# Last stage of an eight-layer kernel: four TensorE waits per block left out, gathered blocks in a ring of 12 instead of 8

## The reference

```python
def _L3_ffn_ref(x, gate_w, gate_bias, w1, w3, w2, sw1, sw3, sw2):
    DIM, INTER, N_EXPERTS, TOPK, N_SHARED = 128, 128, 8, 2, 2
    xt = x.reshape(-1, shape[-1])
    scores = jax.nn.softmax((xt @ gate_w.T).astype(jnp.float32), axis=-1)
    _, idx = jax.lax.top_k(scores + gate_bias, TOPK)
    weights = jnp.take_along_axis(scores, idx, axis=1).astype(x.dtype)
    y = jnp.zeros_like(xt)
    for e in range(N_EXPERTS):
        gate_e = jnp.sum(jnp.where(idx == e, weights, 0.0), axis=1)
        h = jax.nn.silu(xt @ w1[e].T) * (xt @ w3[e].T)
        y = y + gate_e[:, None] * (h @ w2[e].T)
    z = jax.nn.silu(xt @ sw1.T) * (xt @ sw3.T) @ sw2.T
    return (y + z).reshape(shape)
...
    x = x + _L3_ffn_ref(_layernorm(x, axis=-1), L3_ffn_gate_w, ...)
```

## Time and profile before

| | |
|---|---|
| three timed runs | 1195.08, 1190.69, 1195.14 us (median 1195.08) |
| the profiled execution's own time | 1197.03 us |
| its span, first to last instruction | 1195.2 us |
| granted TensorE clock, mean over the span | 0.908 of full speed |
| busy share of the span | PE 80%, DVE 70%, ACT 54%, POOL 39% |
| block loop: transpose of block 0 to that of block 58 | 1072.49 to 1182.25 us |

### The profile page before, as it was taken

How to read it: one execution, slowest core, us unless ns; L and a number is a source line. 1 busy time by engine, 2 the same in 40 slices (tenths; PEclk the granted TensorE clock), 3 DMA queues, 4 the chain that set the end, 5 groups by cost and what they waited for, 6 DMA issues and landing times.

```text
span 1195.2 us, 21237 instructions
## 1 busy us (share of the span) xinstructions
PE 957.0 (80%) x7158; PEld 634.0 (53%) x7158; DVE 831.6 (70%) x2062; ACT 647.2 (54%) x1137; POOL 471.0 (39%) x454
## 2 busy tenths in 40 slices
PE   5868810578988998799759999997979988849997
PEld 3653310554555675455416766666735546428876
DVE  5686699857886674477768999999658885414443
ACT  3424567946652444565347878785456644105443
POOL 6610000001120002345169999998012242554544
PEclk9998965679999999999958999999979998969999
DMA  7000000046000000000000000000000000232331
GB/s 281 1 1 1 1 0 0 1 151 185 2 1 1 1 1 1 1 2 2 2 0 1 2 0 0 0 0 1 1 1 1 2 2 1 72 105 77 99 83 47
DMA packets 24234, 33.77 MB, mean 28 GB/s; under 512 B 3484, under 2 KB 20389, under 8 KB 23888
## 3 DMA queue, kind: packets, MB, share of 16 engines
q1 hardware_dynamic: 20720, 26.20, 7.1%
q0 software_dynamic: 3424, 6.38, 1.5%
HBM read 18.34 MB, written 15.98 MB: 29 GB/s over the span
## 4 chain that ended last, share of the span: by engine, by line
issue 71%; PE 6%; DMA 1%; POOL 1%; SPq 0%; POOLq 0%; DVE 0%; ACT 0%; DVEq 0%
PE psum L2417 3%; PE psum L2435 1%; POOL out L2295 1%; DMA out<-big 1%; DMA big<-rows 1%; PE psum L1443 1%; PE psum L2426 1%; PE psum L2410 0%; SPq L2308 0%; POOLq L2291 0%; DVE big L2616 0%; PE psum L289 0%; PE psum L500 0%; ACT hrow L271 0%; PE psum L519 0%
## 5 line engine op out<-in xcount | busy, mean ns | idle before, releaser
L785 DVE TENSOR_REDUCE hq<-psum 128x16 f32<-128x1024 f32 x96 | 114.4, 1221 | 80.5 <-PE psum L519 43.5
L429 POOL TENSOR_TENSOR big<-big,w_const 128x256 f32<-128x256 f32 x48 | 35.8, 748 | 260.6 <-PE psum L565 227.4
L1975 POOL TENSOR_TENSOR big<-big 128x512 f32<-128x512 f32 x128 | 128.7, 1051 | 21.4 <-ACT big L1880 21.4
L1903 ACT ACTIVATE psum<-big,tmp 128x512 f32<-128x512 f32 x128 | 84.9, 686 | 18.9 <-DVE big L2072 16.2
L2072 DVE SCALAR_TENSOR_TENSOR big<-big,tmp,psum 128x512 f32<-128x512 f32 x128 | 90.4, 744 | 5.5 <-ACT psum L1903 2.5
L675 ACT ACTIVATE big<-psum 128x1024 f32<-128x1024 f32 x64 | 62.0, 1021 | 54.4 <-PE psum L549 54.4
L2606 DVE SCALAR_TENSOR_TENSOR big<-psum,big 128x128 f32<-128x128 f32 x118 | 36.0, 348 | 79.2 <-issue 59.9
L790 DVE RECIPROCAL big<-psum 128x256 f32<-128x256 f32 x48 | 84.0, 1750 | 7.5 <-PE psum L565 7.3
L2295 POOL DMA_INDIRECT out<-big x59 | 57.9, 982 | 64.2 <-issue 33.4
L1443 PE MATMUL psum<-f_downT,tmp 128*128 128x128 f32 x192 | 25.7, 300 | 68.0 <-DVE tmp L1326 68.0
L1985 POOL TENSOR_TENSOR big<-big 128x1024 f32<-128x1024 f32 x32 | 75.3, 2366 | 11.4 <-DVE big L2072 11.4
(11 more groups left out here) (316 smaller groups left out, 2584.5 us busy)
## 6 DMA issues: line engine op xcount, KB each, us to landing
rows<-pad SPq DMA_DIRECT2D x1, 7670.0 KB, 33.4
big<-rows SPq DMA_DIRECT2D x59, 130.0 KB
tmp<-in_pack_f SPq DMA_DIRECT2D x1, 2050.5 KB, 9.1
w_f<-in_pack_f SPq DMA_DIRECT2D x1, 1280.0 KB, 12.7
tmp<-in_pack_once SPq DMA_DIRECT2D x1, 960.0 KB, 8.1
out<-big POOLq DMA_INDIRECT x59
X<-in_x SPq DMA_DIRECT2D x1, 768.0 KB, 5.0
w_a<-in_pack_a SPq DMA_DIRECT2D x3, 256.0 KB, 8.2
```

Source lines behind the costliest of these rows:

```text
L785: dve.tensor_reduce(nm, psum[:, 1 + 2 * t:3 + 2 * t, :].rearrange("p c (r l k) -> p (c r) l k", r=2, k=SK), AX.X, ALU.max, negate=True).th ...
L1903: act.activation(bank(EX_BANK + h % 2), ssum[t][:, h * 512:(h + 1) * 512], ACT.Exp, bias=shift2[:, t * NH2 + h:t * NH2 + h + 1]).then_inc( ...
L1975: ins = pool.tensor_tensor(ssum[t][:, h * 512:(h + 1) * 512].rearrange("p (i j) -> p i j", i=ROWS2), st[:, 0, h, 0:ROWS2].unsqueeze(2).to_ ...
```

## The change

Four waits of TensorE's turn are left out: that of the transpose on `f3_hT`, that of the first matmuls on `f3_hid`, that of the second transposes on `b_hidT`, and that of the last matmuls on `f3_x` (kept for the last block alone). Other waits that TensorE makes earlier in its order imply them: the first matmuls of block j - 2, for instance, already waited for the copy that frees the bank of block j's transpose. The ring of slots and of `out3` tiles grows from 8 to 12, so SP and VectorE wait for the store of block j - 12 instead of j - 8. `slots` may reach 48 words further than before into tiles that are dead by then.

```diff
-        RS = 8
+        RS = 12
-        slots = Carve(6 * GN)
+        slots = Carve(7 * GN)
...
             for j in range(NB3):
                 if j >= RS:
-                    sp.wait_ge(S("b_so%d" % (j % 4)), 16 * (j // 4 - 1))
+                    sp.wait_ge(S("b_so%d" % (j % 4)), 16 * (j // 4 - 2))
...
                     pe.wait_ge(S("b_in%d" % (j % 4)), 16 * (j // 4 + 1))
-                    if j >= 2:
-                        pe.wait_ge(S("f3_hT"), N_GROUPS + j - 1)
                     pe.transpose(bank(j % 2)[:, 0:P], slot3[j % RS][:, 0:P], ident).then_inc(S("f3_tn"), 1)
                 if 1 <= i <= NB3:
                     j = i - 1
                     pe.wait_ge(S("f3_hT"), N_GROUPS + j + 1)
-                    if j >= 2:
-                        pe.wait_ge(S("f3_hid"), 2 * N_GROUPS + 2 * j - 2)
...
                     pe.wait_ge(S("f3_hid"), 2 * N_GROUPS + 2 * j + 2)
-                    if j >= 2:
-                        pe.wait_ge(S("b_hidT"), j - 1)
...
                     pe.wait_ge(S("b_hidT"), j + 1)
-                    if j >= 2:
+                    if j == NB3 - 1:
                         pe.wait_ge(S("f3_x"), N_GROUPS + j - 1)
...
                     if j >= RS:
-                        dve.wait_ge(S("b_so%d" % (j % 4)), 16 * (j // 4 - 1))
+                        dve.wait_ge(S("b_so%d" % (j % 4)), 16 * (j // 4 - 2))
                     dve.tensor_tensor(out3[j % RS], slot3[j % RS][:, XS3:XS3 + P], bank(5 + j % 2)[:, 0:P], ALU.add)\
```

## The result

The changed kernel takes 1180.3 us in the median of six runs (1178.74 to 1183.21), the kernel before 1194.8 beside it (six runs, 1190.38 to 1195.43). The ratio is 0.9894, with a 95% interval of 0.9871 to 0.9916. That is faster by over 0.5%, and 14.5 us less; the forecast was 1182.5, with a range of 1178.5 to 1189. The profiled execution took 1178.74 us. One of all the executions timed for this document, in after_move_b (1454.02 us at a granted clock of 0.632), was in a slower state of the chip and is left out of the ratio.

What follows compares the result with a forecast made beforehand. TensorE was taken to bound the block loop. Waits 8.4 + loads 3.9 + restarts 1.0 = 13.3 us off 1197.03 gave 1183.7, 1181.8 by the runs' median, taken as 1182.5; range 1178.5 to 1189.

Steps and rivals of the forecast that it cites:

- What bounds the kernel: Block loop: TensorE is the bound; 14.5 us above the pace of pure streaming is the most the change can touch.
- The four waits, 8.4 us: TensorE's queue: three waits at 0.1 us delay each of 28 table-read turns by 0.30; the fourth is worth nothing.
- Next to nothing to spare: Turns with the table read: without the waits they become short ones of 1.64 us, the queue barely in time.
- The loads, 3.9 us: TensorE's three waits for a block's load: twelve slots cover GpSimd's drain, so all 3.9 us are gained.
- the restarts, 1.0: After a wait for a load the queue is again some 0.3 us late; three or four of these, about 1 us, go.
- What stays, 1.2 us: Block loop: 1.2 us remain where the table read is longer than 0.30 us or the queue pauses.
- Costs: Whole kernel: nothing is added; SP issues four loads earlier, and the end behind block 58 stays.
- The sum: All terms: 8.4 + 3.9 + 1.0 = 13.3 us off the profiled 1197.03, giving 1183.7.
- the step from 1181.8 to 1182.5: Final time: 1181.8 from the timed runs' median, taken as 1182.5 because a lower run may have less to win.
- The waits are free: Rival, chance 0.11: the table read makes TensorE's gap; only the ring's 4.9 us are gained, 1190 us.
- The ring is still too short: Rival, chance 0.08: block 41 waits for store 29, 2.6 to 3.9 us stay, 1186 us.
- Stores land too late: Rival, chance 0.03: twelve loads in flight slow GpSimd's stores; at 8 us landing, turns of 2.0, 1202 us.

Runs made afterwards that it cites:

- after_move_b: The changed kernel with the table read moved behind the first matmuls, a second time, on the third chip: 1194.44 us, ratio 0.9951 to the kernel before.
- the ladder: Median long turns (those with the table read) with none, one, two or three of the waits on the queue's way present: 1.64, 1.72, 1.83 and 1.97 us.
- back_hidT: The changed kernel with only the second transposes' wait on b_hidT put back: one run, 1189.56 us, loop 95.39.
- waits_only: The kernel before with the four TensorE waits left out, ring still of 8: 1194.86 against 1197.72 us, ratio 0.997.
- ring_only: The kernel before with the ring grown from 8 to 12, all TensorE waits kept: 1194.69 us, ratio 0.9988.
- ring_move: The kernel before with ring of 12 and the table read moved behind the first matmuls, all waits kept: 1189.01 us, ratio 0.993.
- after_move: The changed kernel with the table read moved behind the first matmuls as well, on the first chip: 1190.25 us, ratio 0.9933 to the kernel before.
- after_c: The changed kernel unaltered, measured a third time, on the third chip, against the kernel before: 1192.25 against 1198.46 us, ratio 0.9944.
- ring10: The changed kernel with a ring of 10 slots instead of 12: one run, 1184.72 us, loop 92.98.
- back_x: The changed kernel with only the last matmuls' wait on f3_x put back for the other blocks: one run, 1181.86 us, loop 90.78.
- before: The kernel before the change, nothing altered, in its first profile: profiled execution 1197.03 us, median of six runs 1194.8 us.
- before_again: The kernel before the change, nothing altered, profiled a second time, on the second chip: 1196.57 us, loop 102.25.
- after_again: The changed kernel unaltered, measured and profiled a second time, on the second chip, against the kernel before: 1180.44 against 1193.76 us, ratio 0.990.

## Why the prediction was right, point by point

**What bounds the kernel.** It took TensorE's stream for the bound and 14.5 us for the most that the change can touch. The windows of after have TensorE busy in all of the 89.17 us, and loop and block 58's turn give back 13.9 us of the 14.5. That holds.

**The four waits, 8.4 us.** The lateness of long turns went from 8.2 to 0.6: 7.6 us. The price of 0.1 a wait and its place (three on the way, the fourth for nothing) were forecast from the spacing in the earlier trace rows, and the ladder and back_hidT show both. Small surprise: once they are gone, the table read starts 0.26 behind VectorE, and the first matmuls follow 1.03 us behind it (1084.24 to 1085.27) instead of 1.32, just in time. "Next to nothing to spare" holds: one wait back and 0.05 us is missing. The data don't hold the loop above 1.64 either: the long turns of six kernels run at that.

**The loads, 3.9 us, and the restarts, 1.0.** Both are gone. They were worth a little more: counted as lateness, with the small ones that the waits view leaves out, 4.5 ahead of the transposes and 1.8 in the short turns. That the waits alone would run into the ring was said as well, and waits_only shows it with its 3.19.

**What stays, 1.2 us.** 0.6 stayed, mostly in block 4's turn (1.82) and in turns 22, 38 and 54 (1.74, 1.74, 1.77). The long table read, which was named as one reason, isn't it (last section).

**Costs.** Nothing was added, and nothing shows: the drain is as long, the stores catch up at 1.28 to 1.29 us each, the tail is 12.65 us instead of 12.96.

**The sum.** 13.3 us were forecast and 13.9 came out of loop and block 58. The medians differ by 14.5, and the measured 1180.3 is 2.2 under the forecast: 0.6 from the loop, 0.7 from the step from 1181.8 to 1182.5, the rest not explained. The prediction took the rest of the program as unchanged; the two profiled executions differ there by 4.4 us, so a comparison of these two alone would have overstated the change.

**Where the Trainium skill stood against it.** The Trainium skill gives TensorE a queue of 64 instructions ("TensorE: Matmul & The Clock Gate", architectural detail) and a sequencer that goes on past a waiting matmul ("Perfetto Trace Analysis", tensor engine instruction). By that, waits would be free. In the ladder they are some 0.1 us each, so the trace disagrees, as it did before the change.

**The rivals.** *The waits are free*: refuted by the ladder. *The ring is still too short*: refuted by the load of block 41, issued 5.3 us ahead of its use. *Stores land too late*: nothing of it, the turns are 1.64. What no rival foresaw is that the same change gives 6.2 us on one chip. It would have been measured there as 1192, above the range, so it was luck that the first measurement met no such pause. The turns that the change treats are as forecast there too; what the prediction lacked is a term for a pause that some chips show.

## What to carry to other kernels

Find the instruction at which an engine's queue last stands still in a turn, and count what it must step through from there to the first work that can be late: only on that way do waits and register instructions cost, and moving the longest of them (here the table read) ahead of the stand brings the turns to the same 1.64 us as leaving three waits out. Two causes that limit the same loop must be lifted together, or the second takes up what the first gives (4.4 and 1.9 us alone, 13.6 together, by single profiles from different chips; the 5.8 us of new waits in waits_only show the same within one). And before a gain of one per cent is believed, time both kernels on more than one chip, and split the profile's difference into the part that the change touches and the part it cannot.

## What the runs showed of the hardware that was not expected

**A pause in the middle of the loop, on two of the three chips of the experiments.** Ten profiles have the changed kernel's ring or one of ten, ring_only left aside. In the six from the first and the third chip (ring_move, after_move, after_c, after_move_b, back_hidT, ring10) TensorE, VectorE and ScalarE all stand still once, and turns 38 to 40 are long for it (38 alone in ring10, 38 and 39 in after_move_b), a few us after GpSimd's drain has ended; in the three from the second chip and in the changed kernel's first profile they don't. Ring_only, from the first chip, has a milder disturbance there that lasts longer. After_move in order of time:

```profile
1140.70 0.38 PE L2422 MATMUL psum<-w_const,big 128*128 128x128 f32 x2
...
1140.92 0.61 PE L2431 MATMUL psum<-tmp,big 128*128 x4
...
1141.11 0.39 ACT L2468 ACTIVATE big<-psum 128x256 f32<-128x256 f32 x1 [0.80 <-PE psum L2410]
...
1141.59 0.61 DVE L2602 SCALAR_TENSOR_TENSOR big<-psum,big 128x128 f32<-128x128 f32 x2 [1.04 <-issue]
...
1142.34 0.38 PE L2422 MATMUL psum<-w_const,big 128*128 128x128 f32 x2
1143.38 0.98 POOL L2295 DMA_INDIRECT out<-big  x1 [0.30 <-issue]
1144.00 0.39 ACT L2476 ACTIVATE big<-psum 128x256 f32<-128x256 f32 x1 [2.50 <-PE psum L2422]
...
1144.53 0.71 PE L2431 MATMUL psum<-tmp,big 128*128 x4 [1.80 <-issue]
...
1145.51 0.29 DVE L2612 TENSOR_TENSOR big<-big,psum 128x128 f32<-128x128 f32 x1 [3.31 <-PE psum L2431]
```

Who stops first? The releasers in brackets are inferred and mislead here; each of the engines' instructions is in the trace 59 times (or a multiple), so they can be counted off to their blocks. ScalarE's copy at 1144.00 is that of block 35, whose transposes ended at 1141.08 (1140.70 + 0.38). ScalarE was free at 1141.50 and stood for 2.50 us with its input there. VectorE's addition at 1145.51 is that of block 34, whose matmuls ended at 1141.53; VectorE was free at 1142.20 and stood for 3.31. TensorE, though, waited for ScalarE's copy, which ended at 1144.39, and went on at 1144.53. So it is in all six: an instruction of ScalarE starts 2.5 to 3.3 us after everything it waits for, one of VectorE in three of them (3.31, 1.86 and 1.45 us), and TensorE's stop follows from these. In ring_only the same two engines stand for 1.1 and 1.9 us. In the other seven profiles none of their instructions in the loop is over 0.6 us late in this sense. GpSimd goes on.

Then the granted clock falls, as the windows of this kernel show:

```profile
1141.00:1145.00 4.00, 2.20 (x16) 1.77 (x16) 0.61 (x2) 0.77 (x2) 2.75 (x3) 1.00 0.45 127
1145.00:1150.00 5.00, 4.19 (x17) 3.40 (x16) 2.00 (x7) 2.02 (x7) 1.97 (x2) 0.53 0.37 93
1150.00:1155.00 5.00, 5.00 (x27) 4.32 (x26) 1.70 (x6) 2.03 (x7) 1.97 (x2) 0.78 0.28 77
1155.00:1165.00 10.00, 10.00 (x69) 9.08 (x68) 4.83 (x18) 5.64 (x19) 5.89 (x6) 1.00 0.24 61
```

A TensorE that was busy without a gap at 1.00 (2.4 GHz) idles for some 1.8 us of 4, and the next 5 us run at 0.53, near the lower level (1.2 GHz). The two together cost 6.1 us here (turns of 3.70, 4.13 and 3.14 instead of 1.64), in ring10, where the clock stays at 1.00, 3.6 us. From 1139 to 1143 the DMA view shows packets that load instructions, besides the blocks' and the stores':

```profile
q14 instruction: 2, 0.02, 1.7%
q8 instruction: 1, 0.02, 1.5%
```

An engine that has to wait for its next instructions would explain why ScalarE and VectorE stand with their inputs there. It is not shown: the two packets of q14 lie ahead of 1141, and such a pair stands in turn 36 or 37 of all fourteen profiles, the seven without any such stop among them (in the changed kernel's first profile at 1129.6, behind its drain). No run took them away or moved them, so the cause stays open, and so does what differs between the chips. The place speaks for a part of the drain in it, since the stores catch up there, but back_x, with the same stores and no pause, tells that this isn't enough.

Is the wait of the earlier trace rows the same pause? In the three profiles with a ring of 8 TensorE takes block 37 2.18, 2.07 and 2.24 us after SP issued its load (before, before_again, waits_only), and later blocks that were just in time took 2.13 to 2.18 (43 and 45 in waits_only). Neither ScalarE nor VectorE stands with its inputs there. So this was a wait for data. Whether the kernel before also pauses on the first and the third chip isn't known, as it has no profile there.

**Pauses ahead of the loop.** A stop of the same look makes up 3.9 of the 4.4 us ahead of block 4. In the kernel before, this stands in the scatter of rows, with the releaser shown as "remote"; the changed kernel's profile has no such wait there:

```profile
1045.15 0.69 DVE L2540 TENSOR_TENSOR big<-X,psum 128x512 f32<-128x512 f32 x1 [9.14 <-remote]
```

All eight profiles from the first and the third chip have such a wait, of 10.0 to 11.4 us, with either ring; the four from the second have none. Block 0 starts up to ten us later there than the changed kernel's 1068.14, with the very same kernel (1078.43 in after_c). How much of this the kernel before loses on those chips isn't known. And the place is not the whole story: before_again and after_again have no such wait, and still block 4 stands 4.0 us apart (1079.57 and 1075.57), here because the scatter starts later (1028.27 and 1024.39). The medians of that chip differ by 13.3 us, close to the 13.5 of its loop and tail, so these 4 us seem to be no part of what the change gives.

**Long turns in steps of 16.** What lateness is left in the changed kernel behind block 4's turn falls mostly on turns 22, 38 and 54, in after_again too (1.75, 1.74, 1.77). The table read's duration doesn't explain it (297 to 307 ns from 1100 to 1127, turn 22 among them). In after_move they are gone. What it is was not tested.
